# A decoder layer's walk over head pairs: GpSimd's three rotary operations made in four column parts each

## The reference, cut to what matters

```python
x = x + attention(layernorm(x), ...)      # 4 batches x 512 tokens x 512, 16 heads
x = x + quantised_mlp(layernorm(x), ...)  # int8-like linear layers
x = x + top2_moe(layernorm(x), ...)       # 8 experts
```

```python
q_nope, q_rope = (q[..., :DN], q[..., DN:])
q_rope = q_rope * cos + rotate_half(q_rope) * sin
q = jnp.concatenate([q_nope, q_rope], axis=-1)
scores = jnp.einsum('blhd,bmhd->bhlm', q, k) * scale
attn = jax.nn.softmax(scores, axis=-1)      # after a causal mask
out = jnp.einsum('bhlm,bmhd->blhd', attn, v)
```

## Time and profile before

| | us |
|---|---|
| median of 3 runs (1156.41 to 1159.36) | 1156.94 |
| the profiled execution, its own time | 1159.43 |
| its span, first to last instruction | 1157.6 |
| PE busy | 981.6 (85%) |
| DVE busy | 938.2 (81%) |
| ACT busy | 670.5 (58%) |
| POOL busy | 337.7 (29%) |
| the three rotary lines of POOL, 32 operations each | 44.9 + 40.5 + 37.0 |

### The profile page before, as it was taken

One profiled execution on the slowest core, in us unless ns is written; L12 is line 12 of the kernel. 1 busy time (PEld: TensorE's weight loads), 2 busy tenths in 40 slices (PEclk: granted clock), 3 DMA queues, 4 the chain that ended last, 5 costly groups with the idle time before them and its releaser, 6 DMA issues.

```text
span 1157.6 us, 18702 instructions
## 1 busy us (share of the span) xinstructions
PE 981.6 (85%) x6124; PEld 570.6 (49%) x6124; DVE 938.2 (81%) x2617; ACT 670.5 (58%) x1417; POOL 337.7 (29%) x568
## 2 busy tenths in 40 slices
PE   0346667999999999999999999999979766749997
PEld 0234334555555555555555555555535545525553
DVE  5767748999989988998898888888867886857885
ACT  1446556766666656666666665666623676633442
POOL 1036533223223222322322232222202357521211
PEclk9869779999999999999999999999989988869998
DMA  9300003333333336333335333335352830001334
GB/s 346 148 1 1 1 8 71 65 72 69 67 63 72 62 65 140 65 68 63 66 62 112 89 62 64 67 69 133 62 156 93 251 109 0 2 0 41 88 75 91
DMA packets 217328, 90.78 MB, mean 78 GB/s; under 512 B 191496, under 2 KB 202760, under 8 KB 216720
## 3 DMA queue, kind: packets, MB, share of 16 engines
q1 hardware_dynamic: 217232, 89.58, 33.6%
HBM read 36.06 MB, written 7.34 MB: 37 GB/s over the span
## 4 chain that ended last, share of the span: by engine, by line
PE 59%; DVE 20%; ACT 7%; issue 5%; POOL 5%; DMA 3%; SPq 0%; DVEq 0%; ACTq 0%; POOLq 0%
PE bank L1966 13%; PE bank L1916 8%; PE bank L1951 6%; PE bank L971 5%; PE bank L1864 3%; PE bank L1895 3%; PE bank L980 2%; PE bank L1934 2%; PE bank L1935 2%; PE bank L1936 2%; PE bank L1938 2%; PE bank L1937 2%; DVE arena L1567 2%; DVE arena L1574 2%; DVE scal L1711 1%
## 5 line engine op out<-in xcount | busy, mean ns | idle before, releaser
L1256 ACT ACTIVATE arena<-bank,arena,scal 128x128 f32<-128x128 f32 (+3 forms) x256 | 157.7, 616 | 111.8 <-POOL arena L1097 110.7
L1966 PE MATMUL bank<-arena 128*128 128x512 f16 x768 | 179.2, 381 | 1.9 <-DVE arena L1600 1.9
L1097 POOL TENSOR_TENSOR arena<-arena,scal 128x1 f32<-128x1 f32 x256 | 51.7, 202 | 346.5 <-DVE arena L1550 344.8
L1574 DVE SCALAR_TENSOR_TENSOR arena<-arena 128x128 f16<-128x128 f32 (+3 forms) x256 | 142.1, 555 | 9.1
L1916 PE MATMUL bank<-arena 128*128 128x512 f16 x576 | 137.4, 384 | 0.0
L1567 DVE TENSOR_SCALAR arena<-arena 128x128 f16<-128x128 f32 (+3 forms) x256 | 125.3, 490 | 7.4 <-DVE arena L1559 0.8
L1550 DVE TENSOR_REDUCE arena<-bank 128x1 f32<-128x128 f32 (+3 forms) x256 | 123.6, 483 | 7.8 <-PE bank L1939 6.7
L1951 PE MATMUL bank<-arena 128*128 128x512 f16 (+3 forms) x768 | 119.0, 306 | 11.2 <-DMA arena<-arena 6.0
L1966 PEld LDWEIGHTS bank<-arena 128*128 128x128 f16 x768 | 73.0, 98 | 81.1 <-issue 4.7
L1951 PEld LDWEIGHTS bank<-arena 128*128 128x128 f16 x768 | 72.3, 100 | 63.3 <-issue 17.0
L1275 ACT ACTIVATE arena<-bank 32x512 f32<-32x512 f32 x128 | 75.3, 588 | 26.0 <-PE bank L1895 24.8
(11 more groups left out here) (206 smaller groups left out, 2030.7 us busy)
## 6 DMA issues: line engine op xcount, KB each, us to landing
arena<-in_L_attn_w_qb SPq DMA_DIRECT2D x1, 4608.0 KB, 21.3
arena<-arena SPq DMA_TRANSPOSE x272, 2.7
arena<-in_x SPq DMA_DIRECT2D x4, 1024.0 KB, 6.7
arena<-in_L_attn_w_o SPq DMA_DIRECT2D x1, 4096.0 KB, 31.5
arena<-in_fside_BxS2xS SPq DMA_DIRECT2D x4, 1024.0 KB, 8.5
arena<-in_L_ffn_w SPq DMA_DIRECT2D x8, 512.0 KB, 7.5
out<-arena SPq DMA_DIRECT2D x16, 256.0 KB, 2.4
arena<-in_x SPq DMA_DIRECT2D x12, 256.0 KB, 3.0
```

What stands on the lines that cost most here:

```text
L1256: act.activation(pf(k), banks[S_BANKS[G % 3]][:, 0:n], ACT.Exp, bias=NB[:, k:k + 1], scale=sc_exp, accum_out=SUM[:, k:k + 1]).then_inc(s_e ...
L1574: dve.scalar_tensor_tensor(out=ph_part(k, 1), in0=pf(k).rearrange("p (t c) -> p t c", c=P), scalar=R4[:, k:k + 1], in1=ph_part(k, 0), op0= ...
L1966: last = pe.matmul(banks[Y_BANK][:, :], ot(gp, a, k, (q & 3) * P, P), wo(b, gp * GH + k), start=(k == 0 and n == 0), stop=(k == GH - 1 and ...
```

## The change

GpSimd's three rotary operations are each written as a loop over four column ranges of 128 (P is 128, L is 512). The wait stands before the first part and the increment on the last, so what the others see of it is the same two events. The places in the list, the operands and the other engines' lists are as before. It holds for all 32 pairs, the one made ahead of the walk too. GpSimd gets 9 instructions more for each pair, 288 in all.

```diff
             def rope_sin(i):
 
                 pool.wait_ge(r_swap, i + 1)
-                pool.tensor_tensor(RSW, RSW, SINT, ALU.mult).then_inc(r_sin, 1)
+                for o in range(0, L, P):
+                    last = pool.tensor_tensor(RSW[:, o:o + P], RSW[:, o:o + P], SINT[:, o:o + P], ALU.mult)
+                last.then_inc(r_sin, 1)
 
             def rope_sum(i):
 
                 pool.wait_ge(r_rot, i + 1)
                 pool.wait_ge(r_sin, i + 1)
-                pool.tensor_tensor(RT1, RT1, RSW, ALU.add).then_inc(r_sum, 1)
+                for o in range(0, L, P):
+                    last = pool.tensor_tensor(RT1[:, o:o + P], RT1[:, o:o + P], RSW[:, o:o + P], ALU.add)
+                last.then_inc(r_sum, 1)
 
             def rope_split(i, par):
 
                 pool.wait_ge(r_own, i + 1)
-                pool.tensor_tensor(QR[:, (par * 3 + 2) * L:(par * 3 + 3) * L], RT1, RHI, ALU.subtract).then_inc(r_split, 1)
+                for o in range(0, L, P):
+                    low = QR[:, (par * 3 + 2) * L + o:(par * 3 + 2) * L + o + P]
+                    last = pool.tensor_tensor(low, RT1[:, o:o + P], RHI[:, o:o + P], ALU.subtract)
+                last.then_inc(r_split, 1)
```

## The result

| | before | after |
|---|---|---|
| median, us, five runs each on one chip | 1159.36 (1156.41 to 1161.16) | 1167.81 (1167.35 to 1170.63) |
| the profiled execution's own time and its span, us | 1159.43, 1157.6 | 1167.36, 1165.6 |
| POOL busy, us | 337.7 | 387.6 |

The ratio is 1.0084, with a 95% interval of 1.0063 to 1.0104: slower by 0.84%, some 9.7 us. It compares the means; the two medians lie 8.5 us apart and the two profiled executions 7.9. The forecast was +2.9 us, and 1159.8 us in all on a base of 1156.94, the median of the first three runs before; that of five is 1159.36, so 2.4 us of the distance to 1167.81 is the base.

The account below looks back on a forecast made before the run. TensorE was taken as the fullest engine, so only what makes it wait counts. 0.42 + 1.7 + 0.3 - 0.35 + 0.8 = +2.9 us on 1156.94 gave 1159.8 us, own range 1157.5 to 1162.5, whole range 1155.0 to 1166.0.

Parts of the forecast that it names:

- A part's cost: GpSimd's 128-column operations: 0.41 us from start to start, 0.46 alone, so a run of four 1.69 against 1.27, 0.42 longer.
- The start: Before the walk's first scores: the sine's 0.42 is hidden behind `rotate`, the sum's is not; +0.42 us.
- The late pairs: Pairs 24, 26, 28, 30, without preparation: the sine's 0.42 goes straight through step 4's bias to TensorE; +1.7 us.
- The prepared pairs: Twelve even pairs, 0 to 22: step 4's bias 0.80 later against 0.78 slack; +0.03 for ten pairs, +0.3 us.
- Pair 20: The odd one of the prepared pairs: L1574, just behind the sine, is let in after the first part; -0.35 us.
- The first pairs: Pairs 0 and 2, walk not yet steady: the later bias of step 4 pushes ScalarE and late exponentials; +0.8 us.
- The splits and the odd pairs' runs I cost at nothing: All splits and odd pairs' runs: one to four us of other work covers them before the next pair's scores; 0.
- the three places of the forecast: TensorE's waits: for L1535 before transposes L1873, 7.9 us; for exponentials before scores, six times; four of these in pairs 24-30.
- The one at 1167 us: Rival: GpSimd loses turns to VectorE, step 4's bias comes 1.2 to 1.4 us later; about 1167 us, chance 0.20.
- That VectorE would be set free: Rival: in prepared pairs, VectorE's casts are blocked less and TensorE's transposes come earlier; about 1153.5 us, chance 0.09.
- That GpSimd doesn't let VectorE in between parts: Rival: cast and L1535 end 0.42 later and TensorE waits that longer at L1873; +7.1, 1164 us, chance 0.10.
- that there is nothing to see: Rival: a later wait swallows the late pairs' delay, or parts are cheaper; +0 to +1, 1157.5 us, chance 0.15.

Follow-up runs that it names:

- the even-pairs variant: Against the kernel before, the three rotary operations in four parts only where issued in even pairs, whole elsewhere; ratio 1.0020 [1.0006, 1.0033].

## Why the prediction was wrong

- **A part's cost: right.** The median of a part is 456 ns in the sine, 453 in the sum, 427 in the split, and an undisturbed run of four takes 1.69 us as worked out. The linear fit through 1, 256 and 512 columns held.
- **The start: right.** +0.41 against +0.42, by the sum alone: from the first copy to the first scores it takes 11.50 us with only the sum in parts and 11.08 with only the sine.
- **The late pairs: right.** 0.44 a pair in pairs 26 to 30 instead of 0.42; pair 24 paid nothing (its period is 41.04 against 41.01), so +1.35 instead of +1.7.
- **The prepared pairs: the mechanism right, the size too small.** The bias's chain comes 0.87 late instead of 0.80, on an edge where each tenth counts in full. And the edge of 0.78 was itself too wide by 0.06, since the scores start 0.06 behind the end of the exponentials, which the sum left out. That makes 0.15 before step 7's scores instead of 0.03. The value products behind VectorE's subtraction L1588, 0.16, were not in the sum at all. That is 0.31 a pair instead of 0.03, some 2.2 us over the eight pairs from 6 to 22 without 20. (L1535's end came 0.26 earlier instead of 0.34. The forecast's own sign that it would be longer by 0.15 gives 0.24.)
- **Pair 20: right.** The period of pairs 20 and 21 went from 45.46 to 45.47, but there the odd pairs' +0.44 lies on top. Without that, in the even-pairs variant, it fell to 45.03: -0.43 against -0.35 forecast. VectorE's operation of before's L1574 took 0.98 us in the changed kernel instead of 1.80.
- **The first pairs:** pairs 0 to 5 cost 1.8 us, forecast +0.8 and a little. The three periods moved by +1.15, -0.94 and +1.61; I did not take them apart.
- **The failed step** is "The splits and the odd pairs' runs I cost at nothing: their cover is one to four us of other work before the next pair's scores need them". Of the splits it is right. Of the odd pairs' sine and sum it named the wrong consumer: the scores have that cover, but the bias of step 5 stands behind the sum. Its exponentials push ScalarE and those of step 6, these push VectorE, VectorE is full from there into the next pair, and the first to ask for its work is TensorE's L1864, with 0.20 us of slack. That wait stood in the trace before, once, with 1.5 us, and wasn't among the three places of the forecast. The odd pairs cost +0.44 a period with nothing else changed, and moving the addition took it away. The sentence behind it, that without cover "16 x 0.1 to 0.4 would be added", had the size at its upper end for the nine steady prepared pairs and too much for the late ones, where the odd pairs cost nothing; no rival and no chance stood on it.
- **The rivals.** The one at 1167 us came nearest in time, by luck, and wasn't the cause: it wanted the bias of step 4 1.2 to 1.4 us later, and it was 0.87. What it said of L1567 crossing the parts did happen in the odd pairs (0.74 us instead of 0.49). That VectorE would be set free is true in its own place, and worth 0.30 a pair (L1873 from 3.9 to 1.2 us in nine), but more than that was lost elsewhere. That GpSimd doesn't let VectorE in between parts falls with the cast's 0.49, and that there is nothing to see falls with the late pairs' +0.44 and the interval of the ratio.

By the table of the walk (+9.6 against +2.9), the missed 6.7 us are: pairs 6 to 23, +6.0 measured against about -0.1; pairs 0 to 5, 1.0 more, cause open; late pairs 0.35 less. In pairs 6 to 23 some 4.0 us are the odd pairs' (nine times 0.44) and some 2.1 the even pairs' (eight times 0.28, less 0.08 at pair 20).

## What to carry to other kernels

When an operation on an idle engine gets longer, follow every small operation queued behind it to its consumer, through the engine that has no idle time, until somebody waits: the slack to look for is not at the next reader of the long operation's result but at the first reader of whatever the full engine does next, which may be in the next iteration. Cutting an operation whose event comes with the last part releases nobody sooner; it helps only an engine that is held up while the long operation runs, as VectorE's cast was, and here it paid (0.28 us a period, not seen in the whole time) only once the small operation behind it and the residual addition had been moved ahead. When a forecast ends 0.02 us from an edge, both sides of it belong into the range.

## What the runs showed of the hardware

A VectorE operation that waits gets in between two GpSimd operations, and where one waits, a boundary moves time from one engine to the other; in pair 26, where none waited, the four parts took 1.70 us. In pair 12 the cast went from 0.90 to 0.49 us and L1542 from 0.69 to 0.83, while the run of the sine went from 1.65 (0.38 over its undisturbed 1.27) to 2.71 (1.02 over 1.69). Not every VectorE operation takes part: `rotate` (L1601), which reads PSUM and one operand in SBUF, ran inside that same sine (446.03) in its usual 0.68 us. The Trainium skill, page SBUF — State Buffer, section Who interferes with whom, says that a VectorE instruction with at most one input in SBUF, outside the two-port modes, doesn't contend with GpSimd and that one with two does, where GpSimd's instruction reads SBUF; the 0.68 of `rotate` and the longer L1542 agree with it. It also says that issue order decides which of the two is held, which the cast's two durations, behind a whole sine and between its parts, agree with.

GpSimd's small operations take 0.15 us from start to start with one column and 0.41 with 128 (four in a row took 1.69 to 1.70, the last alone 0.46), so cutting 512 columns into four costs 0.42 us and into two 0.14: each further instruction costs 0.14.
